# Ternary weights' group sums in PSUM banks of their own, copied by ScalarE in two slots

## What is computed

```
x: (32, 128, 512)   ctx: (32, 128, 512)   16 heads of 32
ctx_img = ctx[:, :257]   # all 128 rows; the text part is empty
q = rms_norm(linear(layernorm(x), q_w, q_b), norm_q_w)
k = rms_norm(linear(ctx_img, k_img_w, k_img_b), norm_k_img_w)
v = linear(ctx_img, v_img_w, v_img_b)
x = x + tanh(g_xattn) * linear(attention(q, k, v), o_w, o_b)

scale = clip(mean(abs(wg), 64 at a time), 1e-08)      # w in bfloat16
ternary(w) = clip(round(wg / scale), -1, 1) * scale
h = square(relu(layernorm(x) @ ternary(W_fc).T))      # 2048 wide
x = x + tanh(g_ffn) * (rms_norm(h) @ ternary(W_proj).T)
```

## Time and profile before

| | us |
|---|---|
| median of 3 runs | 1076.02 (1072.2 to 1078.03) |
| the profiled execution | 1075.54 |
| its span, first to last instruction | 1073.5 |
| TensorE busy in the span | 940.4 (88%) |
| ScalarE, VectorE, GpSimd busy | 696.6, 675.9, 625.3 |

### The profile page before, as it was taken

One profiled execution on the slowest core, in us unless ns is written; L12 is line 12 of the kernel. 1 busy time (PEld: TensorE's weight loads), 2 busy tenths in 40 slices (PEclk: granted clock), 3 DMA queues, 4 the chain that ended last, 5 costly groups with the idle time before them and its releaser, 6 DMA issues.

```text
span 1073.5 us, 26220 instructions
## 1 busy us (share of the span) xinstructions
PE 940.4 (88%) x9938; PEld 577.1 (54%) x10038; DVE 675.9 (63%) x1379; ACT 696.6 (65%) x1256; POOL 625.3 (58%) x672
## 2 busy tenths in 40 slices
PE   3364554789999999999999999999999999999997
PEld 1132232455656665666566655656566665666653
DVE  7766576776666666666676666666666666665420
ACT  3654366657676667766766667676677767776654
POOL 1465567755656566555656565666565555656445
PEclk9766768899999999999999999999999999999999
DMA  7423232124232323323333333433223333322110
GB/s 283 138 70 84 64 117 42 31 54 67 70 71 65 57 58 61 70 60 70 70 65 66 67 65 70 70 70 60 50 61 70 63 68 70 67 44 51 31 31 20
DMA packets 150798, 74.07 MB, mean 69 GB/s; under 512 B 136208, under 2 KB 136208, under 8 KB 149136
## 3 DMA queue, kind: packets, MB, share of 16 engines
q1 hardware_dynamic: 150672, 72.38, 30.1%
HBM read 30.67 MB, written 8.39 MB: 36 GB/s over the span
## 4 chain that ended last, share of the span: by engine, by line
PE 42%; ACT 24%; issue 16%; DVE 12%; POOL 3%; DMA 2%; DVEq 0%; ACTq 0%; SPq 0%; POOLq 0%
PE bank L441 9%; ACT bank L768 8%; PE bank L440 7%; PE bank L396 4%; PE bank L397 4%; PE bank L398 4%; PE bank L427 3%; PE bank L428 3%; ACT big L715 3%; PE bank L495 2%; ACT square_out L695 2%; PE bank L474 2%; DVE q_raw L969 2%; ACT p_hi L663 2%; ACT q_rows L677 2%
## 5 line engine op out<-in xcount | busy, mean ns | idle before, releaser
L427 PE MATMUL bank<-ft,w 128*128 128x256 f16 x1024 | 232.9, 275 | 3.1 <-DMA ft<-x_rows 1.6
L428 PE MATMUL bank<-ft,w 128*128 128x256 f16 x1024 | 232.6, 274 | 0.0
L441 PE MATMUL bank<-w,big 128*128 128x512 bf16 x512 | 194.3, 380 | 10.8 <-issue 8.6
L440 PE MATMUL bank<-w,big 128*128 128x512 bf16 x424 | 160.9, 379 | 7.5 <-POOL big L1339 5.4
L1339 POOL TENSOR_TENSOR big<-h_sb,big 128x512 f16<-128x512 f32 x120 | 144.5, 1204 | 31.9 <-ACT big L715 17.1
L887 DVE TENSOR_TENSOR p_lo<-bank,p_hi 128x512 f16<-128x512 f32 x128 | 88.5, 692 | 98.2 <-ACT p_hi L663 98.2
L1349 POOL TENSOR_TENSOR hh_sum<-hh_sum,hh_sb 128x512 f32<-128x512 f32 x112 | 141.9, 1267 | 2.2 <-ACT hh_sb L731 2.2
L1305 POOL TENSOR_SCALAR q_ms<-q_ss 128x1 f32<-128x1 f32 x32 | 7.7, 240 | 232.6 <-issue 221.7
L768 ACT ACTIVATE bank<-bank,log_p,exp_scale 128x512 f32<-128x512 f32 x128 | 95.6, 747 | 64.5 <-PE bank L498 64.5
L709 ACT ACTIVATE h_sb<-bank,relu_scale 128x512 f32<-128x512 f32 x128 | 86.7, 677 | 75.5 <-PE bank L428 75.5
L427 PEld LDWEIGHTS bank<-ft,w 128*128 128x128 bf16 x1024 | 100.7, 98 | 26.7 <-DMA ft<-x_rows 7.0
(11 more groups left out here) (202 smaller groups left out, 2310.6 us busy)
## 6 DMA issues: line engine op xcount, KB each, us to landing
x_sb<-in_x SPq DMA_DIRECT2D x32, 256.0 KB, 3.2
ctx_sb<-in_ctx_t SPq DMA_DIRECT2D x32, 256.0 KB, 3.2
out<-out_sb SPq DMA_DIRECT2D x32, 256.0 KB, 2.0
big<-in_w_fc_t SPq DMA_DIRECT2D x4, 1024.0 KB, 5.1
big<-in_w_proj_t SPq DMA_DIRECT2D x4, 1024.0 KB, 5.2
big<-in_wq_t SPq DMA_DIRECT2D x1, 1024.0 KB, 7.1
...
```

The source lines that it names most:

```text
L427: nc.tensor.matmul(dst[:, half], w, ft[i][:, c, :], start=(c == 0), stop=False)
L428: last = nc.tensor.matmul(dst[:, half], w, ft[i][:, C + c, :], start=False, stop=(c == C - 1))
L440: nc.tensor.matmul(dst[:, :], ht_hi[i][:, row], w2[:, m, :], start=(m == 0), stop=False)
L441: last = nc.tensor.matmul(dst[:, :], ht_lo[i][:, row], w2[:, m, :], start=False, stop=(m == M - 1))
```

## The change

It has five parts.

1. Units per slot become 9, 9, 7, 7 (`UNITS`, `FIRST`), and each engine gets its own list of places, written as `tern_units(t, first, last)`: the places in slots 0 and 1, and those in slots 2 and 3.
2. Group sums go to `up_ps` (even units below 18) or `up_b` (all others). In slots 0 and 1 (units below `RAW` = 18) ScalarE copies the sum from PSUM to `t_scale` (`raw_scale`), and VectorE clips it there, in SBUF. TensorE's group sum n then waits for the copy of unit n-2, in slots 2 and 3 for the clip of unit n-1 as before. The waits of `values` and `project_out` for a clip are gone. The up pieces of slots 2 and 3 all use `up_ps`, with one bank instead of two.
3. The maximum over W_fc's scales no longer comes from the clip: each of units 0 to 15 gets four more matmuls of two columns into `fc_ps` (part of `mix_ps`), and one reduction reads them at the end of slot 1.
4. The product with the mask of odd units except 31, 15 of 32, moves from GpSimd to VectorE (`ternary_final`), two units later in its list. The waits for finished units are per unit.
5. Steps moved: the constants made from `ident` ahead of `weight_max(0)`; `constant_row` ahead of the loop, with its bank; `weight_hi(3)` and `v_hi_of(0)` on ScalarE; context_lo(1) behind p_lo(0); on SP the transpose of k(0) ahead of a weight load; on GpSimd q_norm, k_weight and x_norm ahead of most units of their slot.

```diff
-    TERN = 8
-    PLACES = ((0, 2, 1, 1, 1, 1, 1, 1), (0, 1, 1, 1, 1, 1, 2, 1)) + ((1,) * 8,) * 2
+    UNITS = (9, 9, 7, 7)
+    FIRST = (0, 9, 18, 25, 32)
+    RAW = FIRST[2]
...
+        def up_bank(t, f):
+            return up_b if t >= J and f % 2 == 0 else up_ps
...
         def ternary_bank(n):
-            if n < NU:
-                return up_ps
-            return o_ps if sum(PLACES[n // TERN][:6]) <= n % TERN < sum(PLACES[n // TERN][:7]) else mix_ps
+            return up_ps if n < RAW and n % 2 == 0 else up_b
+        def on_dve(n):
+            return n % 2 == 1 and n < 2 * NU - 1
...
             def ternary(n):                                   # TensorE
                 pe.wait_ge(abs_ready, n + 1)
-                need(pe, tscale_ready, n)
+                if n <= RAW:
+                    need(pe, raw_ready, n - 1 if n < RAW else RAW)
+                else:
+                    pe.wait_ge(tscale_ready, n)
...
+                if n < NU:
+                    for k in range(4):
+                        last = nc.tensor.matmul(fc_ps[:, 8 * n + 2 * k:8 * n + 2 * k + 2], abs_w[n % TABS][:, k * P:(k + 1) * P],
+                                                group_mean[:, 0:P:GROUP], start=True, stop=True)
+                    last.then_inc(fc_cols, 1)
...
-                if t < J:
-                    pe.wait_ge(tscale_ready, TERN * t + sum(PLACES[t][:7]))
...
+            def raw_scale(n):                                 # ScalarE
+                act.wait_ge(gsum_done, n + 1)
+                need(act, tsigned_ready, n - TD + 1)
+                need(act, tmask_ready, n - TD + 1)
+                copy_hi(t_scale[n % TD], ternary_bank(n)[:, :], raw_ready)
...
             def ternary(n):                                   # VectorE
+                if n < RAW:
+                    dve.wait_ge(raw_ready, n + 1)
+                    src = t_scale[n % TD]
+                nc.vector.tensor_scalar(t_scale[n % TD], src, TERNARY_CLIP, None, ALU.max).then_inc(tscale_ready, 1)
...
+            def ternary_final(n):                             # VectorE
+                if n < 0 or not on_dve(n):
+                    return
+                dve.wait_ge(tmask_ready, n + 1)
+                dve.wait_ge(tsigned_ready, n + 1)
+                nc.vector.tensor_tensor(ternary_place(n), ternary_place(n), t_mask[n % TD], ALU.mult).then_inc(tern_dve, 1)
```

More of the change, by code:

```diff
@@ L52, in gated_cross_attention_kernel @@
     TAHEAD = 4
-    assert C == 4 and M == 4 * UP and H == 16 and NT % J == 0 and J * TERN == 2 * NU
+    assert C == 4 and M == 4 * UP and H == 16 and NT % J == 0 and sum(UNITS) == 2 * NU
     stack = ExitStack()
@@ L263, in pairs_before, with up_banks, units, dve_finals @@
             return 2 * g + j // 2 - 1
+        def up_bank(t, f):
+            return up_b if t >= J and f % 2 == 0 else up_ps
+        def up_banks(t):
+            return 2 if t >= J else 1
         def last_slot(t):
             return t == NT - 1
-        def units(t, place, tern):
-            before = TERN * t + sum(PLACES[t][:place]) if tern else 0
-            return range(before, before + PLACES[t][place]) if tern else ()
+        def units(t, first, last):
+            if t >= J:
+                return ()
+            return [FIRST[t] + i for i in (first if t < 2 else last) if i < UNITS[t]]
         def ternary_bank(n):
-            if n < NU:
-                return up_ps
-            return o_ps if sum(PLACES[n // TERN][:6]) <= n % TERN < sum(PLACES[n // TERN][:7]) else mix_ps
+            return up_ps if n < RAW and n % 2 == 0 else up_b
+        def on_dve(n):
+            return n % 2 == 1 and n < 2 * NU - 1
+        def dve_finals(n):
+            return sum(on_dve(i) for i in range(n))
+        def pool_finals(n):
+            return n - dve_finals(n)
         def ternary_place(n):
@@ L538, in constant_row, with tern_units @@
                 for c in range(C):
-                    last = nc.tensor.matmul(mix_ps[:, :], vb_wide[:, c, :], stage[3][:, c * D:(c + 1) * D], start=(c == 0),
+                    last = nc.tensor.matmul(tr_a[:, :], vb_wide[:, c, :], stage[3][:, c * D:(c + 1) * D], start=(c == 0),
                                             stop=(c == C - 1))
                 last.then_inc(wov_done, 1)
-            def tern_units(t, place):
-                for n in units(t, place, t < J):
+            def tern_units(t, first, last):
+                for n in units(t, first, last):
                     ternary(n)
@@ L785, in weight_hi, with raw_scales, tern_units @@
                                      scale=w_scale[:, s:s + 1]).then_inc(w_hi_ready, 1)
-            def tern_units(t, place):
-                for n in units(t, place, t < J):
+            def raw_scales(t, *places):
+                for n in units(t, places, ()):
+                    raw_scale(n)
+            def tern_units(t, first, last):
+                for n in units(t, first, last):
                     ternary(n + TAHEAD)
@@ L868, in _ @@
             k_hi(0)
-            for n in range(TAHEAD):
+            v_hi_of(0)
+            for n in range(2):
                 ternary(n)
-            v_hi_of(0)
             x_hi(1)
+            weight_hi(3)
+            for n in range(2, TAHEAD):
+                ternary(n)
             for t in range(NT):
@@ L1117, in constant_row @@
                 dve.wait_ge(wov_done, 1)
-                chain(nc.vector.tensor_tensor(o_const[:, :], mix_ps[:, :], ob_in[:, :], ALU.add))
+                chain(nc.vector.tensor_tensor(o_const[:, :], tr_a[:, :], ob_in[:, :], ALU.add))
                 chain(nc.vector.tensor_scalar(o_const[:, :], o_const[:, :], gain[:, 0:1], None, ALU.mult))
@@ L1138, in ffn_scales, with tern_units @@
                 nc.vector.tensor_tensor(out_gain[:, :], h_unscale[:, :], gain[:, 1:2], ALU.mult).then_inc(ffn_consts, 1)
-            def tern_units(t, place):
-                for n in units(t, place, t < J):
+            def tern_units(t, first, last):
+                for n in units(t, first, last):
                     ternary(n)
+                    ternary_final(n - 2)
             def slot(t):
@@ L1162, in slot @@
                     hidden_lo((t - 1) // J, (t - 1) % J, 3)
-                tern_units(t, 2)
-                if more:
+                if more and not first:
                     context_lo(t + 1, (t + 1) % 2)
@@ L1167, in slot @@
                     hidden_mean_square(g, j)
-                tern_units(t, 3)
+                if not first:
+                    tern_units(t, (1,), (1,))
                 probs_lo(t, 0)
+                if first:
+                    context_lo(1, 1)
                 if down:
@@ L1254, in _ @@
             k_lo(0)
+            constant_row()
             v_lo_of(0)
@@ L1382, in rows_plus_constant, with tern_units @@
                 nc.gpsimd.tensor_tensor(xb[:, :], x_sb[j][:, :], o_const[:, :], ALU.add).then_inc(xb_ready, 1)
-            def tern_units(t, *places):
-                for place in places:
-                    for n in units(t, place, t < J):
-                        ternary(n)
+            def tern_units(t, first, last):
+                for n in units(t, first, last):
+                    ternary(n)
             def slot(t):
```

183 lines of the change are left out of this document (99 added, 84 removed).

## The result

The changed kernel takes 1059.62 us (median of 4 executions, 1056.54 to 1061.08), the kernel before 1075.62 beside it: a ratio of 0.985, interval 0.9815 to 0.9885. It is faster by 16 us; 26.4 were forecast. The time lies inside the range of 1040 to 1062 and the direction is right, but it is 10.6 us above the predicted value, and above 1055, the upper end of what the forecast had by itself. The profiled execution took 1059.54 us, with a span of 1057.8.

The account below looks back on a forecast made before the run. Before the shift-only stretch, a chain of single steps was the bound, chiefly TensorE waiting for VectorE's clips through one bank. Terms over the stretches summed to -26.4 us, so 1075.5 became 1049, range 1040 to 1062.

Parts of the forecast that it names:

- S(4): Mark: start of slot 4's transposed scores on TensorE; forecast at 201.9 us, with an unchanged rest behind it.
- a): Kernel start to slot 0's transposed scores, 54.5 us: earlier units, fewer units between maxima, set-up moves; -8.3 us.
- b): Slot 0, transposed scores to output projection, 28.7 us: projection's wait goes, warmer projection, two units added; -3.1 us.
- c): Slot 0's output projection to slot 1's transposed scores, 14.4 us: hand-over goes, x1n earlier; -1.3 us.
- d): Slot 1, transposed scores to output projection, 30.2 us: two waits ahead of the projection go, warmer projection; -3.7 us.
- e), g): Output projections of slots 1 and 2 to next transposed scores: two ScalarE pairs and hand-over go; -3.9 and -3.8 us.
- f), h): Slots 2 and 3, transposed scores to output projection: projection's wait stays, k_weighted comes earlier on GpSimd; -1.6 us each.
- i): Slot 3's output projection to slot 4's transposed scores, 12.4 us: seventh group sum waits for a clip; +0.9 (0 to +3).
- Rival 1: Contention slows ten VectorE unit instructions between output projections and next scores by 0.9 each: 9 us go, 1058; chance 0.2.
- Rival 2: More of slots 0 to 3 at TensorE's upper clock, projections 1.6 us cheaper, four more such groups: 1042.5; chance 0.1.
- Rival 3: Another last step takes the place of each clip, only the gain at the start stays: 1067; chance 0.07.
- Rival 4: Slots 0 and 1: ScalarE's 18 raw copies wait for GpSimd's products, 18 x 2.3 = 41.8 us, 1091; chance 0.04.

Follow-up runs that it names:

- pool_masks: The changed kernel with all 32 mask products back on GpSimd, nothing else moved: 1058.24 us, ratio 0.984 to the kernel before.
- x1n_first: The changed kernel with GpSimd's ln_rstd and x1n of slots 0 to 3 ahead of the slot's last units: 1060.23 us, ratio 0.9851 to the kernel before.
- sum_behind_up: The changed kernel with the seventh unit's group sum of slots 2 and 3 behind the feed-forward up piece: 1058.66 us, ratio 0.9833 to the kernel before.
- pool_x1n: The changed kernel with all mask products on GpSimd and x1n ahead of each slot's last units: 1056.75 us, ratio 0.9818 to the kernel before.
- free_products: The changed kernel with VectorE's 15 mask products cut to two columns each, all waits kept: 1054.69 us, ratio 0.9785 to the kernel before.
- setup_only: The kernel before with the changed set-up order alone; banks, clips, units and products as before: 1074.57 us, ratio 0.9968 to the kernel before.

## Why the prediction was right in sign and short in size

The sum of the stretches up to S(4) is -20.2 us instead of -26.4, and the rest is 4.5 us longer instead of equal. The marks say where the 6.3 us ahead of S(4) were lost: S(1) came at 85.2 for 84.9 predicted, O(1) at 111.7 for 111.4, S(2) at 126.1 for 124.6, O(2) at 153.1 for 149.6, S(3) at 169.4 for 163.7, O(3) at 193.8 for 188.6, S(4) at 208.2 for 201.9. So two thirds of it lie in slot 2 (f and g), and the rest in e and i.

**a)** -8.4 for -8.3. Right, with 2.7 of it shown to be the set-up order.

**b)** -6.0 for -3.1 in this trace, but -3.3 to -3.8 in pool_masks, x1n_first and sum_behind_up, whose first 70 us have the same steps but for the products. The step holds: the projection follows the v projection at once. Part of the extra is a v projection at the upper level here (2.75 us) and not there (3.75 to 4.69); that is luck, not the forecast.

**c)** +1.9 for -1.3 (+0.6 in sum_behind_up). This is the step whose mechanism failed. In the sum it cost little here, since b was 2.9 us better: b and c together are -4.1 for -4.4 (-3.1 in sum_behind_up). The same terms stand in e and g. It put the moved product at "+0.3" together with one more unit; the rows show 1.11 of waiting and two products of 1.29 and 1.37 us ahead of the maxima. It put x1n at "-0.5", counting one product less on GpSimd; x1n waited 5.9 us (statistics ready at 73.4, x1n at 79.3), most of it behind products. That these are two limits side by side, x1n_first, pool_masks and pool_x1n show for c and e together.

**d)** -3.7 for -3.7, by way of other steps. The projection of slot 1 did not follow within 0.5 us: it waited 2.01 for at_lo, since VectorE idled 3.09 us for GpSimd's first product, spent 1.29 on its own, and then 1.64 on k_lo (timeline of slot 1):

```profile
105.31 1.29 DVE L1080 TENSOR_TENSOR w<-w,t_mask 128x512 bf16<-128x512 bf16 x1 [3.09 <-POOL w L1434]
106.52 1.64 DVE L1002 SCALAR_TENSOR_TENSOR k_rows<-k_weighted,k_rms,k_rows 128x512 f16<-128x512 f32 x1
...
108.91 0.38 PE L417 MATMUL bank<-wo_hi,at_hi 128*128 128x512 f16 x1 [2.01 <-DVE at_lo L933]
```

In free_products that wait is 0.8 and d is 25.2, but in sum_behind_up, with the same instructions as here, it is 3.64, so this difference is not shown to be the products' width.

**e), g)** -2.7 and -1.6 for -3.9 and -3.8. The hand-over and the pairs of ScalarE went as worked out; the term for x1n, units and products, +0.6 and +0.7, was too small by the same mistake as in c. With both limits off (pool_x1n) e gives -4.6. In g there is a second one: the seventh group sum waits for its clip there too, 2.80 us ahead of the up piece, and the prediction costed that in i alone. Moving it gave 0.9 to 2.3 us in g.

**f), h)** +0.5 and -2.1 for -1.6 each. ScalarE's wait for k_rms is gone, and the wait ahead of the projection was 2.10 instead of the 3 kept. In f the output projection then fell to the lower level, 4.4 us instead of 2.75, which is 1.7 of the 2.1 us by which f missed. The same trace shows g's wait of 2.80:

```profile
148.48 0.38 PE L482 MATMUL bank<-out_sb,group_mean 128*128 128x512 bf16 x1 [2.10 <-DVE t_scale L1068]
148.70 0.38 PE L417 MATMUL bank<-wo_hi,at_hi 128*128 128x512 f16 x1
...
152.76 0.38 PE L419 MATMUL bank<-wo_hi,at_lo 128*128 128x512 f16 x1
155.93 0.44 PE L482 MATMUL bank<-abs_w,group_mean 128*128 128x512 bf16 x1 [2.80 <-DVE t_scale L1068]
```

One bank for the up pieces cost 0.5 us, once: the 0 to +1 was right.

**i)** +2.0 for +0.9, inside its range. The group sum named there did wait, 3.24 us, and 0.99 in sum_behind_up; but S(3) to S(4) is as long in both, so what it costs is not shown.

**Rival 1** was the right mechanism with too small a chance. Ten products at 0.9 us more were its price of 9, and ten did take some 0.95 more; but it had all ten on c, e and g, and of the ten that took 1.29 us or more six lie there and one each in d, f, h and i. That the time came out near its 1058 is in part luck: 4.5 of the 10.6 us missing lie behind S(4), and 1.7 in the clock of one projection. The argument against it was the median mask, 426 ns, at its minimum. That row misled because of the order of the steps. A clip releases GpSimd's next product, and VectorE's mask, right behind the clip, starts before it: the mask is spared and GpSimd's product takes 1.32 us instead of 1.15. A product right behind that mask then finds GpSimd at work; eight of those ten stand so. The two others, at 70.21 and 105.31 us, were released by GpSimd, which went straight on to its next instruction. The sum by the rule of the Trainium skill's page was 1060.5, nearest to the 1059.6 measured; free_products bears out the wait for a whole instruction, but not that ten of them are on the path, which no run shows. The prediction's own signs of being wrong came in two of three cases: the products took 1.3 us or more in ten of 15, and the rest has another length; no idle time of ScalarE ahead of a raw copy is in the trace.

Rival 2 came in part: the output projections of slots 0 and 1 ran at the upper level, as the sum had it, and that of slot 2 fell to the lower. Rival 3 did not come: S(4) is 20.2 us earlier, and only 8.4 of that is stretch a. Rival 4 did not come: between 39 and 210 us ScalarE waited 0.4 us in all for a buffer that a unit had to free. (Its product 18 x 2.3 is 41.4, not 41.8, which changes nothing.)

**The rest.** 4.5 us longer, of which 2.9 are the last down block at the lower level and 1.2 one late transposed load. 17 us close to the end of the kernel before, then of after, with the clock third from the right:

```profile
1056.00:1073.00 17.00, 10.25 (x47) 4.19 (x45) 1.72 (x3) 3.77 (x7) 7.10 (x8) 1.00 0.09 32
...
1040.00:1057.00 17.00, 11.96 (x41) 4.92 (x40) 1.72 (x3) 0.88 (x2) 4.26 (x6) 0.80 0.08 31
```

And setup_only's last 18:

```profile
1056.00:1074.00 18.00, 12.27 (x43) 4.96 (x41) 1.72 (x3) 1.31 (x3) 4.72 (x6) 0.79 0.08 30
```

setup_only has the last block of before, word for word, and shows the same fall; the change is not needed for it. The load of ft issued at 495.62 us, in slot 13, landed 4.8 us later instead of 3.1, and TensorE waited 1.59 for it. Such landings are not new: in the kernel before, six of the 32 loads of ft took 4.5 to 5.0 us, but all in even slots, where TensorE waited less than 0.3 us for them. Eleven of the twelve kernels with the new code have one in slot 13, some in slot 15 too, and each cost a wait of 1.4 to 1.7 us; before and setup_only have none there. Why they moved is open. How the last block ran in the executions without a trace is not known, so how much of the 16 us hangs on it stays open as well.
